# Masked neighbour maxima on one core: the selection, the ranks and the late work moved to other uses

## The chip, the cores and the metric

One Trainium2 chip, one of its cores. The metric is the device time of a launch in microseconds (us). The kernel before took 721.28 us (median of 3 runs, 720.97 to 721.76). A change of 0.2% is about what such a measurement can tell.

## The reference, cut to what matters

```python
h = jnp.maximum(_layernorm(x, axis=-1), 0.0)      # x: 8 x 1024 x 128 f32
# per batch: A = adj (1024 x 1024 int32), X = h, S = 25
mask = A != 0
scores = jnp.where(mask, -jnp.arange(N), -inf)
vals, idx = jax.lax.top_k(scores, S)              # the first 25 neighbours by number
feats = jnp.where((vals > -inf)[..., None], X[idx], -inf)
agg = feats.max(axis=2)
agg = jnp.where((degree <= S)[..., None], jnp.maximum(agg, 0.0), agg)
out = jax.nn.relu(concat([X, agg]) @ W + b)       # W: 256 x 128
return x + out
```

Every row takes the maximum over the features of its first 25 neighbours. The features are not negative (relu), so that a maximum may begin at zero.

## The kernel before, in words

The 8192 rows are done in 16 groups of 512, two groups to a batch. A group is one step of `step(it, u)`; the loop over `it` holds four steps (u from 0 to 3). A step is even where it begins a batch (u = 0, 2) and odd otherwise. All five engines run their own copy of the loop and meet at semaphores; the order of the work on each engine is written out by hand. Four stages of different groups overlap:

- Mask: ScalarE makes 0/1 masks from the adjacency (`make_masks`), SyncE's queue transposes them into `mask_t` (`turn_masks`).
- Selection: for each of K = 8 blocks of 128 neighbours TensorE accumulates prefix counts in the PSUM bank `side` (`place`, lines 557 to 567), ScalarE turns them into `chosen` (`choose`), which is 1 for the first 25. SyncE stores each block to memory and loads all of them back in another order, eight classes by neighbour number modulo 8 (`store_chosen`, `load_picks`).
- Ranks: TensorE counts within each class (`ranks`, two `ring` banks), ScalarE writes `rank` (`stage`). Entries with rank above 4 are "late": ScalarE flags them (`find_late`), SyncE skews them between classes (`skew_late`, 7 DMAs), TensorE ranks them again (`late_ranks`) and counts the most of a class (`count`); VectorE reduces that count (`count_rounds`) and GpSimd turns it into a number of rounds (`fold_count`).
- Maxima: for the ranks 1 to 4 VectorE makes one-hot tiles (`make_hot`), TensorE gathers the features with them into two `picked` banks, two classes at a time (`pick_pair`), and VectorE takes the maximum (`take_pair`). That is 4 ranks x 4 pairs = 16 **uses**. Then come rounds for the late entries (`late_round`, `take_late`), as many as the count says and one more; the trace shows 2 in odd steps and in the last, 3 or 4 in the other even ones. At last TensorE projects into the bank `final`, VectorE adds (L806), SyncE stores.

A step works on uses 4 to 15 of group g, with pieces of other groups hung on uses: ranks of group g + 1, selection of group g + 2 (`RANK_WITH`, `SELECT_WITH`, lines 56 to 59), then the late rounds of g, uses 0 to 3 of g + 1 with its first late ranks, and the projection of g. Six late ranks are done before the next step and two with use 4 (`LATE_EARLY`, `LATE_REST_USE`); four 32-row chains of `count` follow the projection.

The layernorm of the next batch is made during a batch: x_in is loaded in the even step (`load_x`, behind the adjacency of four groups later), its statistics taken by VectorE at uses 13 and 14 (`STATS_USES`), moments at 15; `make_gain` at use 5 of the odd step, `normalize` and `low_part` on GpSimd, `relu_parts` on ScalarE at use 12, transposes of h by TensorE into `side` and `final` (`turn_h`) behind use 15, and 14 skews of h by SyncE (`skew_h`).

SyncE's queue is served in the order of its program. In a step that is: adjacency of g + 4, x_in (even), eight stores of `chosen`, the picks load, the skews of late flags, the mask transposes, the skews of h (odd), the output, xres.

Before the loop, group 0 and group 1 go through the same stages one after another: SyncE transposes masks 0, loads adjacency 1 and 2, stores `chosen` of group 0, loads its picks, transposes masks 1, and so on; masks 1 and 2 are made by ScalarE; group 1's eight placements stand behind group 0's first four uses.

Of the kernel before, what the change touches and what calls it, by code (L numbers as in the profile page):

```python
# [29 lines left out]
P = 128  # L30
# [7 lines left out]
def build(nc, x, adj, W, b, out):  # L38
# [43 lines left out]
    with ExitStack() as ctx:  # L82
# [148 lines left out]
        def _(sp):  # L231
# [53 lines left out]

            def first_picks(i):
# [22 lines left out]
            sp.reg_add(masks_due, masks_due, Q)  # L309
            for q in range(Q):  # L310
                sp.wait_ge(mask_made, q + 1)
                sp.dma_start_transpose(mask_t[:, :, q * P:(q + 1) * P], mask[:, q, :]).then_inc(mask_turned, 16)
            load_adj(1, 1)
            load_adj(2, 0)
            sp.reg_add(chosen_due, chosen_due, K)
            for k in range(K):
                sp.wait_ge(chosen_made, k + 1)
                sp.dma_start(kept_by_block[k], chosen[:, k, :]).then_inc(first_stored[k // HALF], 16)
# [10 lines left out]
            turn_masks()  # L329
# [28 lines left out]
        def _(pool):  # L358
# [30 lines left out]
            others_due = pool.alloc_register("pool_others_due")  # L389
            pool.reg_mov(most_due, 0)  # L390
            pool.reg_mov(others_due, 0)

            def fold_count(s):

                pool.reg_add(most_due, most_due, 1)
                pool.reg_add(others_due, others_due, CHAINS)
                pool.wait_ge(late_reduced, 1)
                pool.wait_ge(late_reduced, most_due)
                for c in range(CHAINS):
                    nc.gpsimd.tensor_scalar(late_other[:, c:c + 1], late_most[c * PART:c * PART + 1, :], LINK * P / 2 - 1, 1.0, ALU.add,  # L400
                                            ALU.max).then_inc(late_folded, 1)
# [10 lines left out]
            def step(it, u):  # L412
                g = g_of(it, u)
                fold_count(u % 2)
                if not at_end(it, u, 1):
                    if u % PER_BATCH == PER_BATCH - 1:
                        normalize(batch_of(it, u + 1))
                        low_part(batch_of(it, u + 1), ((u + 1) // PER_BATCH) % 2)
# [5 lines left out]
        def _(act):  # L424
            act.wait_ge(basics_made, 8)
# [62 lines left out]
            for due in (turned_due, *adj_due):  # L488
                act.reg_mov(due, 0)
# [3 lines left out]
            make_masks(1, range(Q))  # L493
            turned_h(0, 0)
            act.wait_ge(consts_made, 3)
# [5 lines left out]
            for p in range(1, PAIRS):  # L501
                find_late(p, 0, K)
            for k in range(K):
                choose(1, k)
            for k in range(LATE_EARLY):
                stage(K, k, late_rank, late_bias[:, k:k + 1])
            make_masks(0, range(Q))

            def step(it, u):
# [5 lines left out]
                for use in range(PAIRS, USES):  # L515
                    if use == LATE_REST_USE:
                        for k in range(LATE_EARLY, K):
                            stage(at + REST_AT, k, late_rank, late_bias[:, k:k + 1])
# [4 lines left out]
                    if use in LATE_USES and more:  # L523
                        p = LATE_USES.index(use)
                        find_late(p, (u + 1) % 2, at + RANK_AT + 2 * p + 2)
# [19 lines left out]
        def _(pe):  # L545
# [11 lines left out]
            def place(g, k, counted):  # L557

                if k == 0:
                    pe.wait_ge(mask_turned, TURNED * (g + 1))  # L560
                    if counted is not None:
                        pe.wait_ge(late_reduced, counted)
                else:
                    pe.wait_ge(chosen_made, g * K + k)
                    nc.tensor.matmul(side[:, :], rest_w[:, :], mask_t[:, k - 1, :], start=False, stop=True, skip_group_check=True)  # L565
                nc.tensor.matmul(side[:, :], select_w[:, :], mask_t[:, k, :], start=(k == 0), stop=True,  # L566
# [19 lines left out]
            def count(g):  # L586

                for i in range(LINK):
                    for c in range(CHAINS):
                        last = nc.tensor.matmul(side[c * PART:(c + 1) * PART, :], half_ones[:, 0:PART], late_skew[:, LINK * c + i, :],  # L590
                                                start=(i == 0), stop=(i == LINK - 1))
                last.then_inc(count_written, 1)

            def turn_h(batch, first):
                pe.wait_ge(h_made, 2 * batch + 2)
                for n, bank in enumerate((side, final)):
                    if n == 0:
                        pe.wait_ge(chosen_made, K if first else K * (2 * batch + 1))
                    elif not first:
                        pe.wait_ge(result_made, 2 * batch)  # L600
# [23 lines left out]
            def project(g, it, u, new_batch):  # L624
# [5 lines left out]
                if new_batch:  # L630
                    pe.wait_ge(h_turned, 2 * batch_of(it, u + 1) + 2)
                part = u % PER_BATCH
# [29 lines left out]
            for k in range(K):  # L662
                place(0, k, None)
            turn_h(0, True)
            for k in range(K):
# [4 lines left out]
            pe.wait_ge(h_turned, 2)  # L670
            for k in range(K):
                place(1, k, None)
            for k in range(LATE_EARLY):
                late_ranks(0, K, k)
            pe.wait_ge(chosen_made, 2 * K)
            count(0)
# [3 lines left out]
            def step(it, u):  # L680
# [7 lines left out]
                for use in range(PAIRS, USES):  # L688
# [3 lines left out]
                    if use == LATE_REST_USE:  # L692
                        for k in range(LATE_EARLY, K):
                            late_ranks(g, at + REST_AT, k)
                    for k in RANK_WITH[use] if more else []:
                        ranks(g + 1, at + RANK_AT, k)
                    for k in SELECT_WITH[use] if not at_end(it, u, 2) else []:
                        place(g + 2, k, g + 1)
# [29 lines left out]
                if more:  # L728
                    for k in range(4, LATE_EARLY):
                        late_ranks(g + 1, at + LATE_AT, k)  # L730
                    if not at_end(it, u, 2):
                        pe.wait_ge(chosen_made, K * (g + 3))
                    count(g + 1)
# [5 lines left out]
        def _(dve):  # L739
            def first_mask(q):  # L740

                dve.wait_ge(adj_first[q], 16)
                nc.vector.tensor_scalar(mask[:, q, :], adj_in[:, 0, q * N:(q + 1) * N], 0.0, None, ALU.not_equal).then_inc(mask_made, 1)

# [32 lines left out]
            def count_rounds(g):  # L777
                dve.wait_ge(count_written, g + 1)
                nc.vector.tensor_reduce(late_most[:, :], side[:, :], AX.X, ALU.max).then_inc(late_reduced, 1)  # L779
# [34 lines left out]
            for q in range(Q):  # L814
                first_mask(q)
            stats_of(0, range(K))
            moments_of(0)
            make_gain(0)
# [10 lines left out]
            nc.vector.tensor_tensor(rest_w[:, :], ones[:, :], select_w[:, :], ALU.subtract).then_inc(consts_made, 1)  # L829
            dve.wait_ge(weights_loaded, 64)  # L830
# [18 lines left out]
            first_parts()  # L849
            dve.wait_ge(ring_read, K)  # L850
# [6 lines left out]
            def step(it, u):  # L857
# [3 lines left out]
                new_batch = more and u % PER_BATCH == PER_BATCH - 1  # L861
                batch = batch_of(it, u + 1)
                ahead = u % PER_BATCH == 0 and not at_end(it, u, PER_BATCH)

                for use in range(PAIRS, USES):
# [14 lines left out]
                    if use == GAIN_USE and new_batch:  # L880
                        make_gain(batch)
# [29 lines left out]
                finish_group(g, s, 16 * (it * (UNROLL // 2) + u // 2 + 1))  # L911

# [24 lines left out]
```

## Time and profile before

| | |
|---|---|
| median of 3 runs | 721.28 us |
| the profiled execution | 721.64 us |
| its span in the trace | 719.9 us |
| mean granted TensorE clock | 0.974 |
| TensorE matmuls busy | 603.5 us (84%) |
| VectorE busy | 589.2 us (82%) |
| ScalarE busy | 425.4 us (59%) |
| GpSimd busy | 85.6 us (12%) |
| moved by DMA | 118.04 MB, mean 164 GB/s |

Busy shares are averages over the span. Times in rows count from the start of the span. A row of a timeline gives start, duration, engine, source line, output and input, and in brackets the idle time of the engine ahead of it with what released it. Durations overlap a little with the next instruction, so that the distance of two starts is the cost of one.

### The profile page before, as it was taken

To read this page: it belongs to the slowest core of one execution; us is meant where nothing else is said; L and a number is where in the kernel's file an instruction comes from. 1 tells how busy PE (TensorE), PEld (TensorE's weight loads), DVE (VectorE), ACT (ScalarE), POOL (GpSimd) and SP (SyncE) were. 2 spreads that over 40 slices of the span, in tenths; PEclk is the share of its full clock that TensorE was granted. 3 is DMA by queue.
4 is the path that set the end of the run, shared out by engine and by line. 5 is a ranking of instruction groups with operands and counts; after the bars stand their busy time and mean duration, and the time that the engine had idled before them with its cause. 6 is when DMAs were issued, how large, how long until landed. Compare 5 with 4: busy or idle time off the path is not lost.

```text
span 719.9 us, 9712 instructions
## 1 busy us (share of the span) xinstructions
PE 603.5 (84%) x2736; PEld 243.4 (34%) x2736; DVE 589.2 (82%) x705; ACT 425.4 (59%) x579; POOL 85.6 (12%) x134
## 2 busy tenths in 40 slices
PE   0555689998999898989899898989798989998976
PEld 0110234343343333434343333343343434342323
DVE  5221398989989799898989799898989898989986
ACT  0555583868268482687568583777478763856210
POOL 3000000401021100311022100311031100311010
PEclk9996799999999999999999999999999999999999
DMA  9883753656744474555945575566744462231100
GB/s 262 299 233 126 232 198 74 216 169 238 183 146 172 111 270 123 183 178 166 270 135 188 124 254 140 204 185 204 224 175 160 126 210 47 78 142 42 46 15 15
DMA packets 107905, 118.04 MB, mean 164 GB/s; under 512 B 74452, under 2 KB 94167, under 8 KB 103383
## 3 DMA queue, kind: packets, MB, share of 16 engines
q1 hardware_dynamic: 107862, 117.61, 52.2%
q14 instruction: 32, 0.25, 0.1%
q8 instruction: 11, 0.18, 0.1%
HBM read 58.85 MB, written 20.97 MB: 111 GB/s over the span
## 4 chain that ended last, share of the span: by engine, by line
PE 43%; DVE 18%; ACT 13%; issue 10%; DMA 8%; SPq 7%; DVEq 1%; ACTq 0%
PE picked L607 14%; PE picked L608 12%; DVE best L787 6%; PE ring L554 6%; DMA x_in<-in_x_dram 5%; PE side L565 3%; DVE hot L774 3%; PE side L566 3%; DVE best L793 3%; ACT late_rank L445 3%; DVE late_hot L799 3%; SPq L269 3%; ACT late L460 2%; ACT mask L440 2%; ACT chosen L455 2%
## 5 line engine op out<-in xcount | busy, mean ns | idle before, releaser
L787 DVE TENSOR_TENSOR best<-picked,best 128x1024 f32<-128x1024 f32 x224 | 271.0, 1219 | 71.5 <-PE picked L608 70.5
L607 PE MATMUL picked<-hot,h_hi 128*128 128x512 f16 x512 | 198.6, 388 | 21.7 <-DVE best L787 11.3
L608 PE MATMUL picked<-hot,h_lo 128*128 128x512 f16 x512 | 197.5, 386 | 0.0
L607 PE MATMUL picked<-late_hot,hi_skew 128*128 128x512 f16 x344 | 131.5, 382 | 24.6 <-DVE late_hot L799 12.8
L608 PE MATMUL picked<-late_hot,lo_skew 128*128 128x512 f16 x344 | 131.3, 382 | 0.0
L793 DVE TENSOR_TENSOR best<-picked,best 128x1024 f32<-128x1024 f32 x86 | 105.1, 1223 | 16.6 <-PE picked L608 15.5
L445 ACT ACTIVATE late_rank<-ring,late_bias 128x512 bf16<-128x512 f32 x128 | 81.7, 686 | 56.4 <-PE ring L554 53.2
L445 ACT ACTIVATE rank<-ring,late_bias 128x512 bf16<-128x512 f32 x128 | 87.4, 687 | 40.4 <-PE ring L554 39.9
L455 ACT ACTIVATE chosen<-side,bias_cut 128x512 bf16<-128x512 f32 x128 | 87.3, 682 | 35.6 <-PE side L566 35.6
L774 DVE TENSOR_SCALAR hot<-rank 128x4096 f16<-128x4096 bf16 x64 | 88.0, 1377 | 23.2 <-ACT rank L445 23.2
L484 ACT COPY best<-picked 128x1024 f32<-128x1024 f32 x32 | 32.5, 1014 | 118.8 <-PE picked L608 118.8
L607 PEld LDWEIGHTS picked<-hot,h_hi 128*128 128x128 f16 x512 | 50.5, 99 | 112.4 <-DVE best L787 31.3
L400 POOL TENSOR_SCALAR late_other<-late_most 1x1 f32<-1x1 f32 x64 | 14.3, 224 | 526.2 <-DVE late_most L779 522.4
L566 PE MATMUL side<-mask_t,select_w 128*128 128x512 bf16 x128 | 52.7, 412 | 23.4 <-DVE rest_w L829 18.1
L460 ACT ACTIVATE late<-rank,bias_late 128x1024 bf16<-128x1024 bf16 x64 | 68.8, 1136 | 0.0
L608 PEld LDWEIGHTS picked<-hot,h_lo 128*128 128x128 f16 x512 | 50.9, 99 | 50.3 <-issue 3.5
L554 PE MATMUL ring<-picks,half_w 128*128 128x512 bf16 x128 | 50.9, 399 | 18.5 <-ACT late_rank L445 11.2
L799 DVE TENSOR_SCALAR late_hot<-late_rank,numbers 128x2048 f16<-128x2048 bf16 x86 | 63.9, 744 | 0.0
L607 PEld LDWEIGHTS picked<-late_hot,hi_skew 128*128 128x128 f16 x344 | 33.6, 98 | 89.2 <-issue 29.4
L440 ACT ACTIVATE mask<-adj_in 128x1024 bf16<-128x1024 uint32 x60 | 58.3, 1046 | 0.0
L565 PE MATMUL side<-mask_t,rest_w 128*128 128x512 bf16 x112 | 46.2, 413 | 14.0 <-ACT chosen L455 12.6
L554 PE MATMUL ring<-late_skew,half_w 128*128 128x512 bf16 x128 | 42.4, 392 | 3.3 <-ACT late_rank L445 3.1
(73 smaller groups left out, 407.3 us busy)
## 6 DMA issues: line engine op xcount, KB each, us to landing
adj_in<-in_adj_dram SPq DMA_DIRECT2D x15, 2048.0 KB, 7.9
kept<-chosen SPq DMA_DIRECT2D x128, 128.0 KB, 3.3
picks<-kept SPq DMA_DIRECT2D x15, 1024.0 KB, 5.0
late_skew<-late SPq DMA_DIRECT2D x32, 192.0 KB, 2.4
x_in<-in_x_dram SPq DMA_DIRECT2D x8, 512.0 KB, 9.0
xres<-in_x_dram SPq DMA_DIRECT2D x16, 256.0 KB, 2.6
late_skew<-late SPq DMA_DIRECT2D x16, 256.0 KB, 2.6
late_skew<-late SPq DMA_DIRECT2D x32, 128.0 KB, 2.3
```

Of the source, the lines that this page charges most:

```text
L440: nc.scalar.activation(mask[:, q, :], counts, ACT.Sign).then_inc(mask_made, 1)
L445: nc.scalar.activation(dst[:, k, :], ring[k % 2][:, :], ACT.Relu, bias=bias).then_inc(ring_read, 1)
L455: nc.scalar.activation(chosen[:, k, :], side[:, :], ACT.Sign, bias=bias_cut[:, 0:1], scale=-1.0).then_inc(chosen_made, 1)
L460: nc.scalar.activation(late[:, 2 * p:2 * p + 2, :], rank[:, s, 2 * p:2 * p + 2, :], ACT.Sign, bias=bias_late[:, 0:1]).then_inc(late_made, 1)
L554: last = nc.tensor.matmul(ring[k % 2][:, :], w[:, :], m, start=(i == 0), stop=(i == len(terms) - 1))
L566: nc.tensor.matmul(side[:, :], select_w[:, :], mask_t[:, k, :], start=(k == 0), stop=True, skip_group_check=True).then_inc(place_written, 1)
L607: nc.tensor.matmul(dst, hi[:, slot, k, :], onehot, start=start, stop=False)
L608: return nc.tensor.matmul(dst, lo[:, slot, k, :], onehot, start=False, stop=stop)
L774: nc.vector.tensor_scalar(hot[:, (t - 1) % 3, :, :], rank[:, s, :, :], float(t), None, ALU.is_equal).then_inc(hot_made, 1)
L787: nc.vector.tensor_tensor(best[:, half, s, :, :], picked[s][:, :, :], best[:, half, s, :, :], ALU.max).then_inc(picked_read, 1)
L793: nc.vector.tensor_tensor(best[:, s, i, :, :], picked[i][:, :, :], best[:, s, i, :, :], ALU.max).then_inc(late_read[i], 1)
L799: nc.vector.tensor_scalar(late_hot[:, part, :], late_rank[:, part, :], which, None, ALU.is_equal).then_inc(late_hot_made[i], 1)
```

## The change

The selection moves from uses 5 to 12 to uses 8 to 15, the ranks from 4 to 11 to 6 to 13. Four late ranks are done ahead of the step instead of six; numbers 4 to 7 go with uses 4 and 5. `count` goes from behind the projection to uses 6 and 7 of the next step and from the bank `side` to `final`; its reduction moves from use 4 to 8, the first late one-hots from 9 and 11 to 11 and 13. Late flags are made two at a time at uses 14 and 15. relu moves from use 12 to 7, the statistics from 13 and 14 to 9 and 10, the moments from 15 to 12, `make_gain` from use 5 of the odd step to the end of the even one, and `normalize` ahead of `fold_count`. `turn_h` waits for the last selection block of the step.

Before the loop, VectorE makes the constants ahead of masks 0, and makes masks 1 and 2 too. Masks 1 are transposed into the second half of `rank`, behind two of the eight stores of `chosen`; masks 2 behind the picks load. Group 1's placements stand four ahead of group 0's ranks and one behind each of its first four uses. The loads of x_in and of the adjacency keep their places in the loop.

```diff
-    SELECT_WITH, RANK_WITH = spread_over(5, 12), spread_over(4, 11)
-    LATE_EARLY, LATE_REST_USE, COUNT_USE, LATE_HOT_USES = 6, 4, 4, (9, 11)
-    LATE_USES, RELU_USE = (12, 13, 14, 15), 12
-    STATS_USES, MOMENTS_USE, GAIN_USE = (13, 14), 15, 5
+    SELECT_WITH, RANK_WITH = spread_over(8, 15), spread_over(6, 13)
+    LATE_EARLY, LATE_WITH, COUNT_WITH, COUNT_USE, LATE_HOT_USES = 4, {4: (4, 5), 5: (6, 7)}, (6, 7), 8, (11, 13)
+    LATE_USES, RELU_USE = {14: (0, 1), 15: (2, 3)}, 7
+    STATS_USES, MOMENTS_USE = (9, 10), 12
...
+            first_turns(0, mask_t)
             load_adj(1, 1)
             load_adj(2, 0)
+            for k in range(2):
+                first_store(k)
+            first_turns(1, rank[:, 1])
+            for k in range(2, K):
+                first_store(k)
                 if k == K - 2:
                     first_picks(0)
             first_picks(1)
-            turn_masks()
             load_adj(3, 1)
+            first_turns(2, mask_t)
             skew_h(0, 0)
             skew_late(0)
...
             def step(it, u):
                 g = g_of(it, u)
-                fold_count(u % 2)
-                if not at_end(it, u, 1):
+                more = not at_end(it, u, 1)
+                if more and u % PER_BATCH == PER_BATCH - 1:
+                    normalize(batch_of(it, u + 1))
+                fold_count(u % 2 if more else 0, u % 2)
...
-            def count(g):
-
-                for i in range(LINK):
-                    for c in range(CHAINS):
-                        last = nc.tensor.matmul(side[c * PART:(c + 1) * PART, :], half_ones[:, 0:PART], late_skew[:, LINK * c + i, :],
-                                                start=(i == 0), stop=(i == LINK - 1))
-                last.then_inc(count_written, 1)
+            def count(g, i):
+
+                if i == 0:
+                    pe.wait_ge(result_made, g + 1)
+                for c in range(CHAINS):
+                    last = nc.tensor.matmul(final[c * PART:(c + 1) * PART, :], half_ones[:, 0:PART], late_skew[:, LINK * c + i, :],
+                                            start=(i == 0), stop=(i == LINK - 1), skip_group_check=True)
+                if i == LINK - 1:
+                    last.then_inc(count_written, 1)
...
                     if n == 0:
-                        pe.wait_ge(chosen_made, K if first else K * (2 * batch + 1))
+                        pe.wait_ge(chosen_made, K if first else K * (2 * batch + 2))
...
             for k in range(K):
-                place(0, k, None)
+                place(0, k)
             turn_h(0, True)
+            pe.wait_ge(h_turned, 1)
+            for k in range(HALF):
+                place(1, k)
             for k in range(K):
                 ranks(0, 0, k)
             pe.wait_ge(lo_made, 1)
             for use in range(PAIRS):
                 pick_pair(0, use, 0)
-            pe.wait_ge(h_turned, 2)
-            for k in range(K):
-                place(1, k, None)
+                place(1, HALF + use)
...
-                    if use == GAIN_USE and new_batch:
-                        make_gain(batch)
...
                 finish_group(g, s, 16 * (it * (UNROLL // 2) + u // 2 + 1))
+                if ahead:
+                    make_gain(batch_of(it, u) + 1)
```

## Rows read from the trace of the kernel before

**Rows 1.** Timeline of VectorE, the even step of group 6.
```profile
328.10 0.69 DVE L806 SCALAR_TENSOR_TENSOR xres<-final,xres 128x512 f32<-128x512 f32 x1 [0.22 <-PE final L639]
330.26 1.23 DVE L787 TENSOR_TENSOR best<-picked,best 128x1024 f32<-128x1024 f32 x1 [1.47 <-PE picked L608]
...
339.78 0.74 DVE L799 TENSOR_SCALAR late_hot<-late_rank,numbers 128x2048 f16<-128x2048 bf16 x1
...
345.99 0.87 DVE L757 BATCH_NORM_STATS2 stats<-x_in 128x6 f32<-128x128 f32 x4
...
347.90 0.86 DVE L757 BATCH_NORM_STATS2 stats<-x_in 128x6 f32<-128x128 f32 x4
348.68 1.21 DVE L787 TENSOR_TENSOR best<-picked,best 128x1024 f32<-128x1024 f32 x1
...
350.37 1.19 DVE L774 TENSOR_SCALAR hot<-rank 128x4096 f16<-128x4096 bf16 x1
```

**Rows 2.** Timeline of TensorE: start of step 0, end of step 5, start of 6.
```profile
84.37 0.61 PE L566 MATMUL side<-mask_t,select_w 128*128 128x512 bf16 x1 [5.26 <-DMA mask_t<-mask]
...
311.14 0.65 PE L602 MATMUL side<-eye,h 128*128 128x128 f32 x4 [0.71 <-ACT h L471]
...
328.63 0.61 PE L590 MATMUL side<-late_skew,half_ones 128*32 128x512 bf16 x8
329.18 0.39 PE L607 MATMUL picked<-hot,h_hi 128*128 128x512 f16 x1
```

**Rows 3.** Timeline of SyncE's queue: issues, steps 4, 5, 6 and 12.
```profile
252.70 0.33 SPq L239 DMA_DIRECT2D x_in<-in_x_dram  x1
...
314.15 1.12 SPq L245 DMA_DIRECT2D late_skew<-late  x2
...
333.60 0.43 SPq L348 DMA_DIRECT2D out_dram<-xres  x1
...
336.93 0.33 SPq L239 DMA_DIRECT2D x_in<-in_x_dram  x1
...
573.39 0.34 SPq L239 DMA_DIRECT2D x_in<-in_x_dram  x1
```

**Rows 4.** Chain of waits (start, length, what), before the loop and in step 6.
```profile
40.46 0.62 PE ring L554
...
336.93 9.04 DMA x_in<-in_x_dram
```

**Rows 5.** Timeline of VectorE in steps 0, 4, 5 and 12.
```profile
102.24 1.21 DVE L787 TENSOR_TENSOR best<-picked,best 128x1024 f32<-128x1024 f32 x1
...
264.12 0.86 DVE L757 BATCH_NORM_STATS2 stats<-x_in 128x6 f32<-128x128 f32 x4
...
311.61 2.69 DVE L774 TENSOR_SCALAR hot<-rank 128x4096 f16<-128x4096 bf16 x1
...
582.52 0.86 DVE L757 BATCH_NORM_STATS2 stats<-x_in 128x6 f32<-128x128 f32 x4
```

**Rows 6.** The tile x_in over the whole span: issue to landing.
```profile
DMA to landing us min/median/max: 3.9/9.0/10.3
```

**Rows 7.** Timeline of GpSimd in step 5.
```profile
300.37 1.90 POOL L386 TENSOR_TENSOR h<-h,gain 128x1024 f32<-128x1024 f32 x1
311.09 2.13 POOL L375 TENSOR_TENSOR h_lo<-h,h_hi 128x1024 f16<-128x1024 f32 x1 [8.82 <-ACT h L471]
```

**Rows 8.** Timeline of ScalarE in step 5.
```profile
310.92 3.21 ACT L460 ACTIVATE late<-rank,bias_late 128x1024 bf16<-128x1024 bf16 x3
```

**Rows 9.** Busy times and granted clock (PEclk, the seventh figure) of a stretch of step 0.
```profile
84.00:88.00 4.00, 3.63 (x9) 1.40 (x10) 1.22 (x1) 1.37 (x2) 0.00 (x0) 0.50 0.94 344
```

**Rows 10.** DMA issues of the page: KB each, median us to landing.
```profile
kept<-chosen SPq DMA_DIRECT2D x128, 128.0 KB, 3.3
picks<-kept SPq DMA_DIRECT2D x15, 1024.0 KB, 5.0
late_skew<-late SPq DMA_DIRECT2D x32, 192.0 KB, 2.4
```

More of the change, by code:

```diff
@@ L284, in store_chosen, with first_turns, first_store @@
                     sp.dma_start(kept_by_block[k], chosen[:, k, :]).then_inc(chosen_stored, 16)
+            def first_turns(g, turned):
+                for q in range(Q):
+                    sp.wait_ge(mask_made, Q * g + q + 1)
+                    sp.dma_start_transpose(turned[:, :, q * P:(q + 1) * P], mask[:, q, :]).then_inc(mask_turned, 16)
+            def first_store(k):
+                sp.wait_ge(chosen_made, k + 1)
+                sp.dma_start(kept_by_block[k], chosen[:, k, :]).then_inc(first_stored[k // HALF], 16)
             def first_picks(i):
@@ L492, in _ @@
                 choose(0, k)
-            make_masks(1, range(Q))
             turned_h(0, 0)
-            act.wait_ge(consts_made, 3)
+            for k in range(HALF):
+                choose(1, k)
             for k in range(K):
@@ L500, in _ @@
                 first_maxima(0, s, 0)
[L501 to L504, printed above, removed]
+                choose(1, HALF + s)
+            find_late(1, 0, K)
+            choose(1, HALF + 2)
+            find_late(2, 0, K)
+            choose(1, HALF + 3)
+            find_late(3, 0, K)
             for k in range(LATE_EARLY):
                 stage(K, k, late_rank, late_bias[:, k:k + 1])
-            make_masks(0, range(Q))
             def step(it, u):
@@ L515, in step @@
                 for use in range(PAIRS, USES):
[L516 to L518 removed]
+                    for k in LATE_WITH.get(use, ()):
+                        stage(at + REST_AT, k, late_rank, late_bias[:, k:k + 1])
                     for k in RANK_WITH[use] if more else []:
@@ L522, in step @@
                         choose(g + 2, k)
-                    if use in LATE_USES and more:
-                        p = LATE_USES.index(use)
+                    for p in LATE_USES.get(use, ()) if more else []:
                         find_late(p, (u + 1) % 2, at + RANK_AT + 2 * p + 2)
@@ L691, in step @@
                     pick_pair(g, use, slot)
-                    if use == LATE_REST_USE:
-                        for k in range(LATE_EARLY, K):
-                            late_ranks(g, at + REST_AT, k)
+                    for k in LATE_WITH.get(use, ()):
+                        late_ranks(g, at + REST_AT, k)
+                    if use in COUNT_WITH:
+                        count(g, COUNT_WITH.index(use))
                     for k in RANK_WITH[use] if more else []:
@@ L829, in _ @@
             nc.vector.tensor_tensor(rest_w[:, :], ones[:, :], select_w[:, :], ALU.subtract).then_inc(consts_made, 1)
+            for q in range(Q):
+                first_mask(q)
+            stats_of(0, range(K))
+            moments_of(0)
+            make_gain(0)
             dve.wait_ge(weights_loaded, 64)
@@ L849, in _ @@
             first_parts()
+            for g in (1, 2):
+                for q in range(Q):
+                    next_mask(g, q)
             dve.wait_ge(ring_read, K)
```

64 lines of the change are left out of this document (27 added, 37 removed).

## The prediction

> **What bounds the kernel now.** I call the passes through the group loop steps 0 to 15. An even step begins a batch. The start of L806, which ends a step, is the zero of the next step's clock ("+x").
>
> I read VectorE's timeline of step 6 first [rows 1]. L806 starts at 328.10. VectorE then waits 1.47 us for the first pick pair of the step and afterwards hardly waits again: through the uses it is the last to be ready. TensorE's rows of the same place [rows 2] show what it waited for: after the projection TensorE still does two late ranks and the count (8 matmuls from 328.63), and use 4's pairs start at 329.18.
>
> Then SyncE's queue [rows 3]. In the odd step before it the late skews are issued from 314.15, behind them the mask transposes and the 14 skews of h, so that the output store leaves at 333.60 = +5.5; behind it come xres, the adjacency and, at 336.93 = +8.8, x_in of the next batch. The chain of waits [rows 4] runs through just this transfer: 9.04 us until it lands, at 345.97 = +17.9, and L757 (stats) starts at 345.99 [rows 1], in use 13. So before the change x_in arrives exactly when it is needed. That one coincidence decides this forecast, because the change moves the first stats to use 9 and leaves the load where it is.
>
> **The change, part by part.**
>
> *Stats at uses 9 and 10, moments at 12.* Durations by the starts in [rows 1]: a half of stats with its gap 0.79, one take of a pair 1.13 (347.90 + 0.78 of stats to 348.68, and 348.68 to 349.81), moments 0.55 (349.81 to 350.37), a late one-hot 0.66 (its 0.74 less the overlap). Before, what remains after x_in lands is stats, take 14, stats, take 15, moments: 2 x 0.79 + 2 x 1.13 + 0.55 = 4.4. After, it is stats, take 10, stats, take 11, late one-hot, take 12, moments, take 13, late one-hot, take 14, take 15: 2 x 0.79 + 6 x 1.13 + 2 x 0.66 + 0.55 = 10.2. TensorE can be only two pairs ahead (two `picked` buffers), so it can't do this work in the wait. Where x_in's landing binds, the step ends 10.2 - 4.4 = 5.8 us later. VectorE would be ready for those stats at about +10 (start at +1, uses 4 to 9 with one make_hot and the reduce: 6 x 1.13 + 1.2 + 0.7, plus 0.5 of waits), so it waits some 7 us.
>
> Which steps? Steps 2, 6 and 10 are bound by the landing already (5.8 each). In step 4 x_in is issued at 252.70 [rows 3]; with 10.3 us of flight [rows 6], the longest, it is there 1.1 before the stats at 264.12 [rows 5], so 4.7; I give step 8 the same. In step 12 no adjacency is loaded ahead of it: issued at 573.39, landed 3.9 us later, the shortest [rows 3, 6], 5.2 before the stats at 582.52 [rows 5]: 0.6. Sum 3 x 5.8 + 2 x 4.7 + 0.6 = 27.4. Fewer chosen blocks are written during the flight now (selection starts at use 8), which may shorten it: x_in alone takes 3.9, behind 2 MB 9.04; I take 0.5 off each of five: 24.9. The ends: 27.4 with the same flight, and 19 if it shortens by 1.7, a third of what lies between the two.
>
> Could the load leave earlier? Its time is a sum of serial issues from late_made of the odd step: 336.93 - 314.15 = 22.8 us [rows 3], none of which the diff touches.
>
> *Late ranks, count and their queue.* On TensorE 3 + 8 matmuls leave the gap between projection and use 4 (329.18 less about 327.9: 1.2 us) and go, as does the same number of late ranks, under uses 4 to 7, where TensorE has four matmuls (0.87) of picks against VectorE's 1.13. `count` goes from `side` to `final`; the reduce now at use 8 is 4 us after the matmuls. In steps 2 to 12, even, the 1.2 us is swallowed by the wait for x_in. In steps 14 and 15, without stats, it is gained: -1.2 each, -2.4. Ends: 0, and -1.5 each, the whole wait of [rows 1].
>
> *Odd steps.* Three things change. The 1.2 us is gained at the start. POOL's low part ran beside make_hot(1), which took 2.69 instead of 1.19 [rows 1, 5, 7]; that pair is taken apart. But normalize now begins when gain is made, so that its second half (1.90 us on POOL, [rows 7]) falls on make_hot(4) in use 5: the same 1.5 us is paid there. The Trainium skill, "SBUF — State Buffer", on the shared port pair, has the pair as an exclusive lock held for a full instruction; the 2.69 us row agrees, and without that rule the odd step would come out 1.5 better.
> Last, selection's block 7 is now at use 15, behind two late flags on ScalarE (three took 3.21, [rows 8], so 2.1), and turn_h waits for it before it may write `side`. Before, TensorE waited there 0.71 for relu, and wrote from 311.14, +20.0 [rows 2]. Walking the uses (take 15 ends at about +20, chosen 6 at +18.7, the two flags at +20.8, chosen 7 at +21.5) turn_h starts at +21.5, 1.5 later; of this 0.5 to 1.1 reaches the last round, since VectorE was behind before. I take +0.5 for each of 7: +3.5. Ends: -0.4 and +1.1 each, -3 to +8.
> Queued behind the waiting turn_h on TensorE are the late rounds; who waits for them is VectorE. The skews of the late flags start by the same rows at about +23.5 against +23.0: seven issues of 0.63 and 2.4 of landing [rows 3, 10] end at +30.3, before they are needed at +31.
>
> *The beginning.* Before, ranks(0) start at 40.46, when picks land [rows 4], then g 1's eight placements run alone, and step 0 waits for masks 2 (5.26 us idle before 84.37, and then the granted clock is 0.50, the 1.2 GHz level, until 88, [rows 2, 9]). After, four placements stand ahead of ranks(0), four between its pairs, and masks 2 are long turned. But first_turns(1) stands on SyncE ahead of six of the eight stores of chosen, and waits for adjacency 1 and VectorE's masks (about 24), then four transposes of 1.3: stores from about 31, the picks load behind them; and choose(1, 0) waits for all eight stores. I put the start of ranks(0) at R = 45 (41.2 if nothing is held, 47 if the stores land slowly). Then: ranks 6.4, one-hot 1.3, four pairs, placements, copies and flags to late_made 10.8 = R + 18.5; seven skews 4.4; eight stores 2.8 and 3.3 to land; adjacency 4 and x_in behind the 5.0 us picks load [rows 10], landed at R + 41.3 = 86.3. Then the 10.2 us above: use 15 ends at 96.5. Before, it ended with the take at 102.24, at 103.4 [rows 5]. That is -6.9; I give 1 us back for TensorE at 1.2 GHz in the thin stretches: -6. Ends 0 and -11.
>
> **Sum.** 24.9 + 3.5 - 2.4 - 6 = +20.0. On the profiled execution's own 721.64 us (span 719.9) this is 741.6; the median of the runs shown is 0.4 lower. I forecast 741.5.
>
> Beside the sum: TensorE will stand idle some 7 us in each of five steps; after the 5.26 us of [rows 2] it ran at 1.2 GHz for about 4 us [rows 9]. In that stretch it needs 1.7 for a pair and VectorE has 1.7 to 1.9 of work per use, with TensorE two pairs behind its lead: 0 to 1 us each, the upper end +5.
> The Trainium skill, "TensorE: Matmul & The Clock Gate", Part 1, says that the clock is throttled by default and released by activity; the trace agrees in those rows, and by this every one of the five waits would open with slow matmuls.
>
> **The rivals.**
> A. *x_in is in time after all, and the balance wins.* Each even step then ends 1.5 earlier (7: -10.5), odd ones 0.4 earlier (-2.8), the last two -2.4, the beginning -6: 700. It speaks for it that VectorE's only large wait in [rows 1] goes. Against it: the load would have to leave 7 us sooner, at about +1, when the queue still issues skews of h until +5 [rows 3]. It decides the case from an issue before about +2. Chance 0.10.
> B. *The wait is shorter, and late flags bound the odd steps.* x_in's flight at 5.6, two thirds of the way from 9.04 to 3.9: 3.4 off each of five (27.4 - 17 = 10), +3.5, -2.4, -11 at the beginning: 722, that is no change; a little more either way makes it faster or slower. Chance 0.10, half of it for faster, a third for the same.
> C. *The beginning gives nothing*, since SyncE's queue holds the stores (R = 47 and more), and the slow clock costs 1 us in each wait: 24.9 + 8 - 2.4 + 0 + 5 = +35: 757. For it: six stores behind four transposes; against it: step 0 no longer waits for masks 2. Chance 0.15.
> D. The forecast with its bounds, 730 to 752: chance 0.65.
>
> **How the numbers follow.** A change of 0.2% (1.4 us) is what a measurement can tell here. Faster: A and half of B, 0.15; same 0.03; slower 0.82. The range takes D, most of C, and the upper part of B: 726 to 757.
>
> **What would show it.** Right: L757 at use 9 in even steps with an idle of 5 to 8 us released by the x_in DMA, 25 to 40 us over the page, x_in issued at about +8.5; matmuls of 0.6 us after it. In odd steps make_hot at use 5 with 2.5 us, the one after use 15 with 1.2, and side's transposes of h released by chosen. At the start, place of g 2 without a wait for the transposes, and L806 of step 0 near 117 instead of 122.67. Wrong: stats without a wait, or x_in issued before +4; then rival A. An L806 of step 0 after 122 speaks for C.

## The result, and the profile after

The changed kernel takes **759.92 us** (median of 4 runs, 758.6 to 763.4) against 721.52 us (4 runs) of the kernel before in the same job: ratio 1.0535, 95% interval 1.0495 to 1.0576, slower. The forecast was 741.5 us, range 726 to 757. The direction was right, the size about half of the real one, and the time lies outside the range. The rows below are of one profiled execution of each kernel; that of the changed kernel took 763.4 us, the longest of its four.

The page of the profile after: the span, part 1 and the clock of part 2.

```profile
span 761.3 us, 9693 instructions
PE 614.4 (81%) x2736; PEld 250.3 (33%) x2736; DVE 592.9 (78%) x713; ACT 418.3 (55%) x571; POOL 70.2 (9%) x134
PEclk9997999998999989998999979999899999999998
```

VectorE has hardly more work than before (592.9 us, 589.2 before), and a smaller share of the span: of the 41.4 us by which the span grew (761.3, 719.9 before), all but 3.7 are idle time of VectorE. The mean granted clock is 0.951, before 0.974. The waits view of the kernel after (engine, instruction, what it waited for: us in total, times, longest) names the place:

```profile
DVE stats L777 <- DMA x_in<-in_x_dram: 45.5, 8, 9.5
PE side L621 <- ACT chosen L473: 15.3, 8, 2.1
```

The statistics wait 45.5 us in all for x_in, against 1.9 before. VectorE's timeline of step 6 after, the answer to [rows 1] (L806 of before is L826 here; the one at 339.07 ends step 5 and is the zero of step 6):

```profile
339.07 0.69 DVE L826 SCALAR_TENSOR_TENSOR xres<-final,xres 128x512 f32<-128x512 f32 x1 [0.21 <-PE final L659]
339.93 1.23 DVE L807 TENSOR_TENSOR best<-picked,best 128x1024 f32<-128x1024 f32 x1 [0.17 <-PE picked L627]
...
347.80 1.21 DVE L807 TENSOR_TENSOR best<-picked,best 128x1024 f32<-128x1024 f32 x1
355.57 0.87 DVE L777 BATCH_NORM_STATS2 stats<-x_in 128x6 f32<-128x128 f32 x4 [6.56 <-DMA x_in<-in_x_dram]
...
362.54 1.23 DVE L807 TENSOR_TENSOR best<-picked,best 128x1024 f32<-128x1024 f32 x1 [0.71 <-PE picked L627]
```

The wait of 1.47 us at the head of the step is gone (0.17), and 6.56 us of waiting for x_in stand in use 9. The last row is a wait of another kind, 7 us behind the landing: VectorE waits for slow matmuls, as shown further down. The issues on SyncE's queue around it, answering to [rows 3]:

```profile
322.64 1.12 SPq L245 DMA_DIRECT2D late_skew<-late  x2
...
342.99 0.43 SPq L358 DMA_DIRECT2D out_dram<-xres  x1
...
346.30 0.33 SPq L239 DMA_DIRECT2D x_in<-in_x_dram  x1
```

The load leaves at +7.2 here (346.30 - 339.07), between +7.2 and +9.5 in all even steps, and takes 9.26 us. The table has distances of L806 to L806, in us, from VectorE's timelines. "Early x" and "early x, flags last" are two of the experiments below:

| step | before | after | early x | early x, flags last |
|---|---|---|---|---|
| L806 of step 0 at | 122.67 | 114.53 | 113.49 | 113.7 |
| 1, 3, 5 | 37.1, 37.0, 37.0 | 40.2, 40.4, 40.3 | 38.6, 38.8, 38.6 | 37.3, 37.5, 37.4 |
| 7, 9, 11, 13 | 37.0, 36.9, 37.0, 37.0 | 38.6, 38.6, 38.6, 40.3 | 39.9, 39.9, 39.9, 38.7 | 37.4, 37.3, 37.3, 37.5 |
| 2, 4 | 46.0, 48.4 | 51.9, 51.8 | 42.8, 42.7 | 42.8, 42.7 |
| 6, 8, 10 | 41.0, 43.2, 41.5 | 47.5, 50.4, 49.6 | 38.8, 38.8, 38.8 | 38.8, 38.8, 38.9 |
| 12 | 45.0 | 48.1 | 42.9 | 42.8 |
| 14, 15 | 38.5, 31.7 | 36.9, 30.4 | 36.9, 29.5 | 36.9, 29.9 |

After less before: beginning -8.1, odd steps 1 to 13 +18.1, even steps 2 to 12 +34.2, steps 14 and 15 -2.9: together +41.3, the growth of the span but for rounding.

### The profile page after: what moved, and what is told of

It is laid out like the page before. It is cut to its first block, busy times and chain, and to the rows that moved or that the text cites. A ratio compares the mean times of both kernels' runs of the same rounds, so it can differ in the third digit from the quotient of the medians.

```text
span 761.3 us, 9693 instructions
## 1 busy us (share of the span) xinstructions
PE 614.4 (81%) x2736; PEld 250.3 (33%) x2736; DVE 592.9 (78%) x713; ACT 418.3 (55%) x571; POOL 70.2 (9%) x134
## 4 chain that ended last, share of the span: by engine, by line
PE 38%; SPq 16%; DMA 13%; ACT 12%; DVE 10%; issue 10%; ACTq 0%; DVEq 0%
PE picked L626 13%; PE picked L627 12%; DMA x_in<-in_x_dram 8%; SPq L269 5%; PE ring L572 5%; SPq L245 4%; DVE best L807 4%; SPq L247 3%; ACT late L478 3%; PE side L582 3%; DVE late_hot L819 3%; ACT mask L458 2%; ACT chosen L473 2%; PE side L583 2%; DMA adj_in<-in_adj_dram 2%
## 5 line engine op out<-in xcount | busy, mean ns | idle before, releaser
L807 DVE TENSOR_TENSOR best<-picked,best 128x1024 f32<-128x1024 f32 x224 | 270.6, 1218 | 30.9 <-PE picked L627 30.4
L626 PE MATMUL picked<-hot,h_hi 128*128 128x512 f16 x512 | 201.0, 393 | 65.6 <-DVE best L807 56.3
L627 PE MATMUL picked<-hot,h_lo 128*128 128x512 f16 x512 | 200.4, 391 | 0.0
L626 PE MATMUL picked<-late_hot,hi_skew 128*128 128x512 f16 x344 | 134.6, 391 | 13.4 <-issue 5.9
L627 PE MATMUL picked<-late_hot,lo_skew 128*128 128x512 f16 x344 | 134.3, 391 | 0.0
L583 PE MATMUL side<-mask_t,select_w 128*128 128x512 bf16 x120 | 49.2, 410 | 17.1 <-DMA mask_t<-mask 17.1
L626 PEld LDWEIGHTS picked<-late_hot,hi_skew 128*128 128x128 f16 x344 | 34.2, 99 | 78.8 <-issue 30.2
L572 PE MATMUL ring<-picks,half_w 128*128 128x512 bf16 x128 | 52.6, 413 | 2.3 <-ACT rank L463 1.2
L458 ACT ACTIVATE mask<-adj_in 128x1024 bf16<-128x1024 uint32 x52 | 50.6, 1055 | 0.0
L582 PE MATMUL side<-mask_t,rest_w 128*128 128x512 bf16 x105 | 44.0, 419 | 7.9 <-ACT chosen L473 6.8
L777 DVE BATCH_NORM_STATS2 stats<-x_in 128x6 f32<-128x128 f32 x64 | 13.8, 279 | 45.5 <-DMA x_in<-in_x_dram 45.5
```

Of the source, the lines that this page charges most:

```text
L458: nc.scalar.activation(mask[:, q, :], counts, ACT.Sign).then_inc(mask_made, 1)
L572: last = nc.tensor.matmul(ring[k % 2][:, :], w[:, :], m, start=(i == 0), stop=(i == len(terms) - 1))
L582: nc.tensor.matmul(side[:, :], rest_w[:, :], turned[:, k - 1, :], start=False, stop=True, skip_group_check=True)
L626: nc.tensor.matmul(dst, hi[:, slot, k, :], onehot, start=start, stop=False)
L627: return nc.tensor.matmul(dst, lo[:, slot, k, :], onehot, start=False, stop=stop)
L807: nc.vector.tensor_tensor(best[:, half, s, :, :], picked[s][:, :, :], best[:, half, s, :, :], ALU.max).then_inc(picked_read, 1)
```

## The experiments

Theory T: x_in's landing binds the even steps; behind each wait TensorE runs at 1.2 GHz and costs more; in the odd steps the transposes of h wait for the last `chosen`, behind two late flags, and all of that delay is paid. Each alternative stands with its run.

**Load x_in earlier.** The change, with the load of the next batch but one issued in the odd step:

```diff
-                if u % PER_BATCH == 0 and not at_end(it, u, PER_BATCH):
-                    sp.wait_ge(normed_made, batch_of(it, u) + 1)
-                    load_x(batch_of(it, u) + 1)
+                if u % PER_BATCH == PER_BATCH - 1 and not at_end(it, u, PER_BATCH + 1):
+                    sp.wait_ge(normed_made, batch_of(it, u) + 2)
+                    load_x(batch_of(it, u) + 2)
```
(and x_in of batch 1 ahead of the loop)

> The changed kernel, with one edit: x_in of the batch after next is loaded in the odd step, as soon as normalize has read x_in (the first one before the loop), instead of in the even step behind the skews of h and the output. Theory 1 (the even steps wait at use 9 for x_in, whose load stands late in SyncE's queue): the wait of 45.5 us before the statistics falls under 3 us, the six even steps each lose their excess over before (34 us in all) and 1.2 more each, the slow matmuls behind the wait go: 712 to 722 us. Rival 1 (selection and ranks at the later uses overload TensorE and ScalarE at the end of the uses, whatever x_in does): still above 745 us.

Measured 704.42 us, ratio to before 0.9748 (0.9711 to 0.9785): 55 us under the kernel after, and below what was expected. In the loop the statistics no longer wait. Step 6 of this run, VectorE:

```profile
314.98 0.69 DVE L828 SCALAR_TENSOR_TENSOR xres<-final,xres 128x512 f32<-128x512 f32 x1 [0.21 <-PE final L661]
...
324.85 0.86 DVE L779 BATCH_NORM_STATS2 stats<-x_in 128x6 f32<-128x128 f32 x4
```

The statistics start at +9.87 (predicted: VectorE ready at about +10). All even steps of a kind are now alike. From the first statistics to L806 it takes 28.97 us in steps 6, 8, 10 and 32.88 in 2, 4, 12, against 23.12 and 27.03 before: +5.85, where the prediction had 5.8.

**Load early in the kernel before.** The same edit, nothing of the change.

> The kernel before, with x_in loaded in the odd step behind the adjacency load and nothing else changed. Theory (in the kernel before x_in lands just when the statistics want it, so its load costs nearly nothing there): 718 to 721, no statistics wait for x_in. Rival (the early load gains by itself what the load-early form of the change gained, from transfers that collide less): 5 to 15 us faster, 706 to 716.

718.94 us, 0.9963 (0.9942 to 0.9984). The load alone is worth 2 us; what the run above gained, it gained since the change needs the data sooner. This kernel also gives the even steps a clean comparison: 44.8, 48.8, 40.9, 43.1, 40.9, 45.0. The change's order of work, with the early load in both kernels, takes 2.0 to 2.1 off steps 2, 6, 10 and 12, and 6.0 and 4.3 off steps 4 and 8. In the kernel with the early load alone, steps 4 and 8 lose their time in the first uses: in step 4 VectorE waits 2.65 us for the first pick pair (1.47 in step 2), then 1.44 and 0.74 for the third and fourth, and the statistics start at +21.74 instead of +17.77:

```profile
243.95 1.22 DVE L789 TENSOR_TENSOR best<-picked,best 128x1024 f32<-128x1024 f32 x1 [2.65 <-issue]
...
250.11 1.23 DVE L789 TENSOR_TENSOR best<-picked,best 128x1024 f32<-128x1024 f32 x1 [1.44 <-PE picked L610]
```

Here the last late ranks go one by one between TensorE and ScalarE, which idles 1.83 us ("issue") ahead of one of them, and 1.63 in step 8; in the kernel before it idles 1.59 and 1.63 in the same place of these steps. No other step of the two runs has such a wait. With these ranks under the uses it doesn't occur, and steps 4 and 8 are as long as the others of their kind. Steps 4 and 8 begin passes of the loop, but so does 12, which is not longer; what the issue wait is stays open.

**The beginning alone**, in the kernel before (shown in part; VectorE's masks 1 and 2 and the constants ahead of masks 0 belong to it):

```diff
+            for k in range(2):
+                first_store(k)
+            first_turns(1, rank[:, 1])
+            for k in range(2, K):
+                first_store(k)
...
+            first_turns(2, mask_t)
```

> The kernel before, with only the new beginning: constants first, masks 1 and 2 by VectorE, masks 1 transposed behind two stores, group 1's placements four ahead of the ranks and one behind each of four uses. The loop is that of before. Theory: the beginning's gain is its own, 8 us as in the changed kernel's trace (L806 of step 0 at 114.5 instead of 122.7): 711 to 716 us. Rival: the gain in the changed kernel came from step 0's other order of late ranks and selection, and with the old loop the first step waits as before: 719 to 722 us.

712.38 us, 0.9862 (0.9824 to 0.9901), inside the expected range. L806 of step 0 is at 116.35 instead of 122.67, so 6.3 of the change's 8.1 us come with the beginning alone:

```profile
116.35 0.69 DVE L826 SCALAR_TENSOR_TENSOR xres<-final,xres 128x512 f32<-128x512 f32 x1 [0.21 <-PE final L652]
```

**Statistics late**, in the change:

```diff
-    STATS_USES, MOMENTS_USE = (9, 10), 12
+    STATS_USES, MOMENTS_USE = (13, 14), 15
```

> The changed kernel with the statistics back at uses 13 and 14 and the moments at 15; the load of x_in stays where it is. Theory 1: x_in lands at +17 to +18 of an even step, which use 13 now waits for by 1 to 3 us, and what follows the landing is 4.4 us of VectorE as before the change; even steps as long as before, 722 to 730 us. Rival 1 (the later uses are overloaded): above 745 us.

717.67 us (9 runs, 715.93 to 724.83), 0.9955 (0.9925 to 0.9986). This one line gives back 42 us (759.92 - 717.67), more than the whole change had lost (38). The expectation was 5 us too high: it took the even steps to be as long as before, and together they are 10.5 us shorter (254.5 against 265.0). The odd steps keep their loss (277.0 against 258.9). The wait is down to 5.3 us in all:

```profile
DVE stats L777 <- DMA x_in<-in_x_dram: 5.3, 5, 2.1
```

**Late flags last**, in the change: the four late flags at use 15, behind the last `chosen`.

```diff
-    LATE_USES, RELU_USE = {14: (0, 1), 15: (2, 3)}, 7
+    LATE_USES, RELU_USE = {15: (0, 1, 2, 3)}, 7
```

> The changed kernel, with the four late flags made behind the last selection block at use 15 instead of two ahead of it. Theory 2 (the transposes of h wait for chosen, which stands behind two late flags, 2.04 us in each odd step): that wait falls to about 0, each odd step would lose 1.6 to 3.3 us. But by theory 1 the load of x_in is timed by SyncE's queue, which starts from the same last late flag: what the odd steps gain the even ones wait longer, and only steps 11 and 13 keep it. Together: 752 to 758 us, with the wait of the statistics grown from 45.5 to 55 or more. Rival 2 (odd steps are longer because normalize on GpSimd blocks make_hot(4), 2.5 us): the odd steps stay as long as they are, no change in either.

755.68 us, 1.0445 (1.0392 to 1.0498). Odd steps fall to 37.3 to 37.5, and the wait for x_in grows from 45.5 to 52.9 (55 or more was expected): what the odd step gives back, the even one waits. With the early load that can't happen:

> The change, with x_in loaded in the odd step behind its adjacency load, and all four late flags at use 15. The time of the run with the early load alone was 704.42. Theory (in odd steps the transposes of h wait for chosen, which stands behind two flags on ScalarE, and this makes them 38.6 to 39.9 long instead of 37.4): seven odd steps each lose 1.2 to 2.5, since no x_in wait takes the gain back now: about 692, with no wait of the transposes of h for chosen over 0.9 us. Rival (the odd step's length comes from VectorE's own work, make_hot beside normalize, and the move of the flags only seemed to help because x_in took up the slack): 703 to 705.

**692.13 us** (692.09 to 692.35), 0.9614 (0.9586 to 0.9643), the theory's number, and the best version here. One odd step of the kernel after (step 7, clock 1.00), where TensorE waits for `chosen`, then VectorE for the first late round:

```profile
408.18 0.66 PE L621 MATMUL side<-eye,h 128*128 128x128 f32 x4 [2.05 <-ACT chosen L473]
```
```profile
411.45 1.22 DVE L813 TENSOR_TENSOR best<-picked,best 128x1024 f32<-128x1024 f32 x1 [3.44 <-PE picked L627]
```

and step 9 of the last kernel, the same two instructions:

```profile
446.80 0.66 PE L623 MATMUL side<-eye,h 128*128 128x128 f32 x4 [0.78 <-ACT chosen L475]
```
```profile
450.02 1.23 DVE L815 TENSOR_TENSOR best<-picked,best 128x1024 f32<-128x1024 f32 x1 [2.13 <-PE picked L629]
```

1.27 us less of TensorE's wait, 1.31 less of VectorE's, 1.3 less in the step.

**One-hot later.** As the last kernel, with `make_hot` of the next rank at use 7, clear of `normalize` on GpSimd:

```diff
-                    if use == 5:
+                    if use == 7:
```

> As the kernel with early load and all flags at use 15, and make_hot of the next rank at use 7 instead of 5, behind the end of normalize on GpSimd. Theory (VectorE's one-hot is held up by GpSimd's pass, 2.53 us instead of 1.22, and VectorE binds the odd steps): that row falls to about 1.2 in odd steps, each is 1.3 shorter, seven of them 9: 9 us less than the kernel it is derived from, about 683. Rival (the 1.3 us is hidden, since VectorE waits for TensorE later in the odd step): the row falls but the time stays within 2 us. Ends: the one-hot is made later than its first pick pair can start, and each step loses up to 1 us.

A miss: 697.59 us, 5.5 slower than the kernel it comes from. The row did fall in the odd steps, from 2.54 to 1.22 us:

```profile
435.31 1.22 DVE L796 TENSOR_SCALAR hot<-rank 128x4096 f16<-128x4096 bf16 x1
...
440.26 1.23 DVE L809 TENSOR_TENSOR best<-picked,best 128x1024 f32<-128x1024 f32 x1 [0.87 <-PE picked L629]
```

but the odd steps stayed at 37.3 to 37.5: the 1.3 us went into waits for TensorE such as the 0.87 shown, and both kernels wait the same 2.13 before the first late round. Even steps grew by 0.7: in them the one-hot had stood in a gap in which TensorE was not ready, and with it gone VectorE waits there:

```profile
393.13 1.23 DVE L809 TENSOR_TENSOR best<-picked,best 128x1024 f32<-128x1024 f32 x1 [0.31 <-PE picked L629]
394.65 1.22 DVE L809 TENSOR_TENSOR best<-picked,best 128x1024 f32<-128x1024 f32 x1 [0.29 <-PE picked L629]
```

(step 8 of this run). So the collision on the one-hot is real, and costs nothing in this kernel: TensorE, not VectorE, sets the first half of a step once x_in is in time.

**The clock behind a wait.** The change, with 24 more matmuls at use 11 of steps 2, 6 and 10 alone, which TensorE runs while VectorE waits for x_in:

```diff
+                    if use == 11 and u == 2 and not at_end(it, u, 2):
+                        pe.wait_ge(late_reduced, g + 1)
+                        for i in range(24):
+                            nc.tensor.matmul(final[:, :], half_ones[:, :], late_skew[:, 0, :], start=True, stop=True)
```

> The change, with 24 additional matmuls into the bank final at use 11 in steps 2, 6 and 10 alone; their result is overwritten and the output stays. They keep TensorE busy about 5 us of the wait for x_in. Theory (behind the wait TensorE runs at 1.2 GHz and this holds VectorE up by 1 to 2 us in each even step): steps 2, 6 and 10 are 1 to 2 shorter than without the fillers (51.9, 47.5 and 49.6 there), the granted clock in them is 0.98 or more, the time about 755. Rival (what follows the wait is held by something else): the clock rises but steps 2, 6 and 10 keep their lengths within 0.4, time 759 to 761; or the fillers themselves are in the way, and these steps are longer.

756.05 us, 1.0497 (1.0445 to 1.0550). By the length of steps the expectation fails (54.2, 47.8, 47.8), since the landing of x_in moves from run to run by more than the effect, and the clock did not reach 0.98 in steps 2 and 6. Counted from the first statistics to L806 it shows in step 10, where the clock held, and this led to a second run with 36 of them:

> The change, with 36 instead of 24 additional matmuls into the bank final at use 11 of steps 2, 6 and 10; their result is overwritten. In the run with 24 TensorE still idled 3.98 us behind them in step 2, and the granted clock was 0.57 in the 6 us after the landing, against 3.46 us idle and 1.00 in step 10. From the first statistics to the end of the step it took 34.90 in step 2 (32.88 without any wait) and 28.98 in step 10 (28.97 without). Theory (what the wait costs beyond itself is TensorE's clock): with 36 the idle time is under 2 us in each of the three, the clock 0.98 or more behind it, and from the first statistics to the end steps 2, 6 and 10 take 32.9, 29.0 and 29.0, while steps 4 and 8 keep 34.6 and 30.5 or more. Rival (step 10 was short by chance, or for another reason such as where x_in landed): step 2 stays at 34.5 or more with the clock at 1.00.

755.34 us, 1.0447 (1.0405 to 1.0489). TensorE's first pick pair behind the landing in step 2, in the kernel after and with 36 more:

```profile
174.06 0.61 PE L626 MATMUL picked<-hot,h_hi 128*128 128x512 f16 x1 [7.12 <-DVE best L807]
```
```profile
174.56 0.39 PE L626 MATMUL picked<-hot,h_hi 128*128 128x512 f16 x1 [0.74 <-DVE best L811]
```

Windows of 6 us from the landing on; columns: window, length, busy us of PE, PEld, DVE, ACT, POOL, the granted clock (the seventh figure), DMA share, GB/s. The kernel after, steps 2 and 6:

```profile
172.00:178.00 6.00, 3.94 (x10) 1.47 (x11) 6.00 (x19) 1.37 (x2) 0.00 (x0) 0.50 0.12 43
...
355.60:361.60 6.00, 3.97 (x10) 1.49 (x11) 6.00 (x19) 1.37 (x2) 0.00 (x0) 0.55 0.07 25
```

with 24 more, steps 2 and 10:

```profile
172.90:178.90 6.00, 3.93 (x10) 1.45 (x11) 5.98 (x19) 1.38 (x2) 0.00 (x0) 0.57 0.04 15
...
531.80:537.80 6.00, 3.62 (x16) 1.35 (x17) 6.00 (x19) 2.02 (x4) 0.00 (x0) 1.00 0.07 26
```

with 36 more, steps 2 (filled) and 4 (not filled):

```profile
172.50:178.50 6.00, 4.94 (x23) 1.73 (x21) 5.99 (x19) 2.01 (x4) 0.00 (x0) 1.00 0.17 59
262.90:268.90 6.00, 3.94 (x10) 1.47 (x11) 6.00 (x19) 1.37 (x2) 0.00 (x0) 0.50 0.04 14
```

| from first stats to L806 (idle of TensorE ahead; clock) | step 2 | 4 | 6 | 8 | 10 |
|---|---|---|---|---|---|
| no wait (early x) | 32.88 | 32.88 | 28.96 | 28.97 | 28.97 |
| after | 34.64 (7.12; 0.50) | 34.60 | 30.97 (6.38; 0.55) | 30.91 | 31.17 |
| 24 more in 2, 6, 10 | 34.90 (3.98; 0.57) | 34.95 | 29.69 (2.81; 0.72) | 30.45 | 28.98 (3.46; 1.00) |
| 36 more in 2, 6, 10 | 32.89 (0.74; 1.00) | 34.66 | 30.02 | 30.09 | 30.00 |

Where the clock stays at 2.4 GHz, the 1.7 to 2.2 us behind the wait vanish to the hundredth (steps 2 with 36, 10 with 24). Step 4, left alone in the same runs, keeps them, and so does step 2 with 24, which has the additional matmuls but a clock of 0.57: the clock counts, not the matmuls as such. Step 12 of the two runs agrees without any: there the statistics waited 1.3 us, the clock read 1.00, and the rest took 32.92 and 32.89 (32.91 with no wait). With 36, steps 6 and 10 are 1.0 longer for a reason of their own: x_in landed earlier there (+16.1), and the additional matmuls, 7.93 us, were still running (the clock is 1.00). The second expectation had missed this. Its step 8, not filled, took 30.09, a little under the 30.5 expected: what an unfilled wait costs behind itself varies, from 0.9 to 2.3 us over the kernel after and the runs with fillers or with the flags last.

## Why the prediction was right or wrong

The profiled execution grew by 41.4 us where the sum had 20.0. Two steps of the sum failed. 14.6 us of the difference lie in the odd steps, where the delay of `turn_h` was taken to be mostly hidden; 9.3 lie in the even steps, where the slow clock behind a wait was kept beside the sum at 0 to 1 us. The beginning and steps 14 and 15 gave 2.6 more than predicted.

*That x_in binds, and what a bound step costs: right.* The statistics wait 7.3, 7.3, 6.6, 9.5, 8.5 and 4.0 us in steps 2 to 12 ("some 7"; step 12 was not expected to wait so long), and 5.85 us more work stands behind the landing (predicted 5.8), shown by the early load.

*Even steps, 24.9 predicted, 34.2 measured.* The growth splits as follows. More work behind the landing: 6 x 5.85 = 35.1. The statistics' start against before: -1.4, -4.2, -1.4, -0.6, +0.1, -3.9, together -11.4; the prediction had -9.9 in this place (-0.5 for the flight in five steps, -1.1 in steps 4 and 8, -5.2 in 12). The single terms were off, as the flight did not shorten in these five (8.85 to 10.03 us against 9.04) and as in step 4 VectorE, not x_in, had set the start before; the sum was not. Behind the wait, beyond these: 1.8, 1.7, 2.0, 1.9, 2.2, 1.2 = 10.8, less 0.3 that before had itself. **This last term is what failed**: "0 to 1 us each, the upper end +5", and it was kept beside the sum. The fillers show that it is TensorE's clock. The mistake was to compare 1.7 us for a pair with 1.7 to 1.9 of VectorE's work per use: the pair is only four matmuls, and TensorE also owes a rank and two placement matmuls per use. Its seven matmuls from 174.06 to 177.02 in step 2 take 3.0 us per use, at 0.43 each, and VectorE's work is 1.8 to 1.9. Here the Trainium skill, "TensorE: Matmul & The Clock Gate", Part 1 (the clock is throttled by default and released by activity), gave the term its sign, and the rows bear it out: 0.50 to 0.72 behind the six waits of the kernel after. [rows 9] had the rate; in the prediction both stood aside.

*Odd steps, +3.5 predicted, +18.1 measured: the larger error.* The path was right: `turn_h` starts at +21.64 in step 3 (228.28), predicted +21.5, behind `chosen`; the one-hot beside `normalize` takes 2.54, as predicted 2.5, and what the Trainium skill, "SBUF — State Buffer", says on the shared port pair was the right rule for the row. That the odd step would come out 1.5 better without the collision is not borne out: in the last kernel the row falls to 1.22 and the step keeps its length. What failed is "of this 0.5 to 1.1 reaches the last round, since VectorE was behind before. I take +0.5". Before, in step 7, the transposes start at 389.11 and VectorE takes the first late pair at 392.36, 3.25 later; after, 408.18 and 411.45, 3.27. The rows of before:

```profile
389.11 0.65 PE L602 MATMUL side<-eye,h 128*128 128x128 f32 x4 [0.71 <-ACT h L471]
```
```profile
389.58 2.69 DVE L774 TENSOR_SCALAR hot<-rank 128x4096 f16<-128x4096 bf16 x1
392.36 1.23 DVE L793 TENSOR_TENSOR best<-picked,best 128x1024 f32<-128x1024 f32 x1
```

The `make_hot` that ended at 392.3 before hid no slack at all: both engines were ready in the same moment. So the whole 1.6 was paid in seven steps (+11.5). On top, in steps 1, 3, 5 and 13 the granted clock falls behind the 2.0 us wait, and the first late round runs slow:

```profile
228.00:234.00 6.00, 5.36 (x20) 2.46 (x21) 0.92 (x2) 6.00 (x8) 0.00 (x0) 0.72 0.56 172
408.00:414.00 6.00, 5.31 (x27) 2.66 (x28) 2.56 (x4) 6.00 (x9) 0.00 (x0) 1.00 0.50 143
```

(the kernel after, steps 3 and 7). In step 3 `turn_h` starts at 228.28, the clock reads 1.00 until about 229.9 and 0.50 from 230 to 233, a matmul starts every 0.43 us instead of every 0.22, and VectorE takes the first late pair 4.91 behind `turn_h` instead of 3.27:

```profile
228.28 0.66 PE L621 MATMUL side<-eye,h 128*128 128x128 f32 x4 [2.04 <-ACT chosen L473]
...
230.39 0.63 PE L626 MATMUL picked<-late_hot,hi_skew 128*128 128x512 f16 x1
```
```profile
233.19 1.23 DVE L813 TENSOR_TENSOR best<-picked,best 128x1024 f32<-128x1024 f32 x1 [5.08 <-PE picked L627]
```

These are the 40.3 us steps, 1.7 above the 38.6 of the others: 4 x 1.7 = +6.8. The sum 11.5 + 6.8 = 18.3 meets the 18.1. With the flags last, the wait is 0.78, no odd step shows the drop, and all seven take 37.3 to 37.5. That the clock does it is read from rows; no run forced the clock to stay in an odd step with the 2 us wait kept. But the other traces settle most of it. The kernel after, early x, statistics late and the two with fillers all keep the wait (2.04 to 2.13 us), in 35 odd steps together. In 20 of them the 6 us from `turn_h` on have the clock at 0.72, and these take 39.9 to 40.4 us; in 15 it is 1.00, and 14 of these take 38.6 to 38.75 (the last, step 13 of statistics late, 39.3). Which steps those are changes from run to run: 1, 3, 5 and 13 after, 7, 9 and 11 with early x. So how much of the 6.8 us an execution pays is chance; the 1.6 us per step are not.

*Steps 14 and 15: right*, -2.9 against -2.4.

*The beginning: right, a little small*, -8.1 against -6. The ranks of group 0 start at 45.29 (R = 45) and the first statistics of the loop at 85.50 (86.3 predicted). From there to L806 it takes 29.03 us, and 29.01 in the run with the early load: the 1 us given back for a slow clock was not paid; the landing gave 0.8 more. The 86.3 itself is not the sum of the terms written down, which reach R + 29.0 with the eight stores and name only 5.0 of the remaining 12.3; the load left at R + 28.9 and took 11.3.

*The rivals.* C had nearly the right total (757) by a wrong sum: its beginning didn't occur, its clock term and its bound of +8 for odd steps did, and these were too small. Rival A's mechanism (the order itself is a gain, 700) came true once x_in was in time: 704.4, and 692.1 with the flags last as well. It had 1.5 per even step where the runs show 2.1 to 6, and odd steps 0.4 shorter, which are 0.4 longer than before even with the flags last. Rival B's shorter flight did not occur.

## What to carry to other kernels

When an edit moves a consumer earlier, look up when its data lands before anything else, and move the load with it: here the same change is 5% slower than before with the load where it was, 2.5% faster with the load moved, and 3.9% with the flags too. A delay is free only if the profile shows idle time that absorbs it; two engines that become ready together have none. Price each new idle stretch of TensorE twice: for itself, and for the matmuls behind it, at what all of its work per use takes at the lower clock.

## What was not expected of the hardware

- The clock fell behind an idle time of only 2.04 us (step 3, 0.72 over 6 us) and held behind 2.05 (step 7), and in the run with 24 fillers fell behind 2.81 and 3.98 and held behind 3.46. Idle time alone doesn't decide it; these runs don't show what does.
- The same late skews, issued right behind the picks load, land in 4.9 us (median) instead of 2.4 [rows 10]; the picks load itself takes 6.5 (5.0 before), while the stores of `chosen` got faster, 1.7 (3.3 before):

```profile
kept<-chosen SPq DMA_DIRECT2D x128, 128.0 KB, 1.7
picks<-kept SPq DMA_DIRECT2D x15, 1024.0 KB, 6.5
late_skew<-late SPq DMA_DIRECT2D x32, 192.0 KB, 4.9
x_in<-in_x_dram SPq DMA_DIRECT2D x8, 512.0 KB, 9.1
```

- In the same place the four mask transposes take 6.52 us on SyncE's queue in step 5, against 5.38 in the kernel before; this holds everything behind them, x_in's load among it. Why they take longer no run here shows.
